# Node tiles of a two-layer graph network moved in small steps under its first layer, with a rebuilt first stage and a new layout of window sums

## The reference

```python
# layer 0: node-projected features are gathered by src, weighted by an edge MLP, summed by dst
f_s, f_v = project(x, Wl1_0, Wl1_1)                    # sc_s, sc_v: the same with Wsc0, Wsc1
w = gelu(gelu(ea8 @ Wfc1 / 8**.5) @ Wfc2 / 8) @ Wfc3 / 8          # 192 per edge: w0, w1, w2, w3
mid0, mid1 = w0*gs*y0, w3*(gv . y1)/3**.5              # gs, gv = f_s[src], f_v[src]; y = edge_attr_4
mid2, mid3 = (w1*gs)[..., None]*y1, w2[..., None]*gv*y0
mid_s, mid_v = segment_sum([mid0 mid1]), segment_sum([mid2 mid3])   # by dst, / 32**.5
res = sc + (mid_s @ Wa) * out(mid_s, mid_v)            # out: the projections Wl2_s, Wl2_v
x = layernorm(x + res)
# layer 1: s, v projected per node, gathered by dst, weighted by relu(ea64 @ W1) @ W2 (224),
# combined with the edge's unit direction (dot, outer and cross products), summed by src
agg = segment_sum(tp, src) / 32
fs, gate, gv = silu, sigmoid and gated vectors of agg @ W_out + skip
x = layernorm(x + concat(fs, gv))
```

## Time and profile before

| | us |
|---|---|
| median of 3 runs | 2745.41 (2740.61 to 2756.41) |
| the profiled execution | 2767.32 |
| its span in the trace | 2765.5 |

### The profile page before, as it was taken

One profiled execution on the slowest core, in us unless ns is written; L12 is line 12 of the kernel. 1 busy time (PEld: TensorE's weight loads), 2 busy tenths in 40 slices (PEclk: granted clock), 3 DMA queues, 4 the chain that ended last, 5 costly groups with the idle time before them and its releaser, 6 DMA issues.

```text
span 2765.5 us, 80992 instructions
## 1 busy us (share of the span) xinstructions
PE 2655.6 (96%) x24330; PEld 2250.7 (81%) x24330; DVE 1649.6 (60%) x4264; ACT 899.5 (33%) x2015; POOL 2063.6 (75%) x1856
## 2 busy tenths in 40 slices
PE   4799999999999999999999999999999999999996
PEld 2477777777777777979999999999999999999993
DVE  5365555556555555526666666666666666666664
ACT  1111111111111112224444444444444444444442
POOL 3477777777777775247888888888888888888884
PEclk9999799889989898659999999999999999999998
DMA  4343343333433333247888888888888888888877
GB/s 132 111 110 105 100 109 106 100 104 105 108 103 105 105 105 85 104 173 142 141 144 144 141 144 143 144 143 143 143 142 143 143 144 142 144 144 142 144 124 189
DMA packets 388993, 355.59 MB, mean 129 GB/s; under 512 B 60992, under 2 KB 340928, under 8 KB 388416
## 3 DMA queue, kind: packets, MB, share of 16 engines
q0 software_dynamic: 150528, 141.40, 34.9%
q1 hardware_dynamic: 234816, 209.69, 27.2%
q10 hardware_dynamic: 3616, 4.11, 0.6%
HBM read 244.75 MB, written 135.90 MB: 138 GB/s over the span
## 4 chain that ended last, share of the span: by engine, by line
PE 65%; POOL 16%; issue 11%; DMA 3%; DVE 1%; DVEq 0%; ACT 0%; SPq 0%; POOLq 0%; ACTq 0%
POOL gat L693 15%; PE ps_o L1062 13%; PE ps_w L1050 12%; PE ps_d L1071 10%; PE ps_o L1060 9%; PE ps_x L1084 6%; PE ps_g L909 4%; PE ps_x L1024 3%; DMA gat<-f,gidx 2%; PE ps_w L935 2%; PE ps_h L928 1%; PE ps_h L923 1%; PE ps_r L981 1%; DMA tab<-summed,sidx 1%; PE ps_y L998 1%
## 5 line engine op out<-in xcount | busy, mean ns | idle before, releaser
L740 POOL DMA_INDIRECT tab<-summed,sidx x784 | 1218.6, 1554 | 264.5 <-issue 212.7
L693 POOL DMA_INDIRECT gat<-f,gidx x784 | 751.8, 959 | 244.8 <-issue 232.0
L1291 DVE TENSOR_TENSOR prod<-ps_w,xg 128x768 f32<-128x768 f32 x392 | 375.4, 958 | 244.5 <-PE ps_w L1050 226.7
L1062 PE MATMUL ps_o<-ro_v,prod 128*128 128x96 f32 x3136 | 478.5, 275 | 0.0
L1062 PEld LDWEIGHTS ps_o<-ro_v,prod 128*128 128x128 f32 x3136 | 413.3, 192 | 0.0
L1050 PE MATMUL ps_w<-hid,wf 64*128 64x128 f32 x4704 | 369.3, 290 | 2.0 <-ACT hid L864 2.0
L863 ACT ACTIVATE xg<-ps_x 128x768 f32<-128x768 f32 x392 | 296.3, 808 | 198.8 <-PE ps_x L1084 189.4
L1050 PEld LDWEIGHTS ps_w<-hid,wf 64*128 64x128 f32 x4704 | 294.1, 188 | 70.2 <-issue 44.6
L1071 PE MATMUL ps_d<-msg,same 128*128 128x193 f32 x1568 | 332.5, 334 | 0.7 <-ACT summed L882 0.7
L1060 PE MATMUL ps_o<-ro_s,prod 96*128 96x96 f32 x1568 | 330.2, 292 | 0.6 <-DVE msg L1302 0.6
L909 PEld LDWEIGHTS ps_g<-sel,ta 128*128 128x128 f32 x1568 | 210.0, 209 | 95.0 <-issue 59.2
(11 more groups left out here) (198 smaller groups left out, 3416.9 us busy)
## 6 DMA issues: line engine op xcount, KB each, us to landing
src_bc<-in_src_rows SPq DMA_DIRECT2D x196, 256.0 KB
tabw<-feat SPq DMA_DIRECT2D x784, 36.0 KB
ea<-in_ea SPq DMA_DIRECT2D x196, 128.0 KB
feat<-fst SPq DMA_DIRECT2D x25, 576.0 KB, 2.9
gat<-f,gidx POOLq DMA_INDIRECT x784
hot_dst<-in_dst_rows SPq DMA_DIRECT2D x98, 128.0 KB
hot_dir<-sh_rows SPq DMA_DIRECT2D x98, 128.0 KB
dst_bc<-hot_dst SPq DMA_DIRECT2D x196, 64.0 KB
```

Source lines behind the costliest of these rows:

```text
L693: pool.indirect_dma_start(out=gat[:, r % 4, k, :], out_offset=None, in_=t["f0"], in_offset=bass.IndirectOffsetOnAxis(ap=gidx[:, r // 4, at ...
L740: pool.indirect_dma_start(out=t["tabs"][into[k]], out_offset=bass.IndirectOffsetOnAxis(ap=sidx[:, r, k:k + 1], axis=0), in_=summed[:, r, k ...
L1062: last = pe.matmul(ps_o[:, k, 96 + 64 * c:192 + 64 * c], prod[:, ur % 2, k, 1 + c, :], ro_v[:, c, :], start=True, stop=True)
L1291: dve.tensor_tensor(prod[:, r % 2, :, :, :].rearrange("p k c e -> p k (c e)"), ps_w4[:, :, 0:3 * P], xg[:, r // 2, r % 2 * 2:r % 2 * 2 + 2 ...
```

## The change

*Node tiles under the first layer.* The loops of PE and DVE in `fast()` take eight groups a step (`PER`), of which the first three steps are peeled. In each, one node tile is done in pieces: DVE copies its sums out of the accumulator (`node_parts`, r = 5, one step ahead), PE projects them (`update`, r = 0), DVE updates `xres` and computes the inverse root by a bit trick and three Newton steps, as a chain of linked one-column operations (`node_update`, `node_scale`, `node_norm`, r = 0, 1, 2), PE transposes and projects (r = 4, r = 6), DVE copies the rows out of PSUM (`node_turned`, `node_staged`). ACT spreads rows into `fst` in steps 2, 3, 4 of the next eight, and stores them to `feat` from its own queue. So tiles 0 to 22 are done within the loop. Of the last two, the sums follow the loop, and the rest stands in the peeled first steps of the second layer: norms at s = 0, transposes after the first gather, projections at s = 1 and 2, ACT's spreading at s = 3 and 4. SP stores the skip rows there (8 DMAs at g = 0, 2 at g = 1), and POOL's scatter of u = 1 waits for them; the tables are taken in a rotated order. One join is left. A tile may be read once no later group adds to it; `check_order` therefore adds to `win_ok` that each group's first target lies within 48 rows of an even spread.

*Sums.* One accumulator `acc` of five parts takes the place of three; DVE forms a dot product and a product with `y` itself (`vy`, `wy`, `dot`), so that `window_sums` has two products instead of three, and `add_window` one add instead of three.

*Unread matmuls.* At r = 1 of each eight groups PE issues four matmuls of 512 columns whose result is never read (`HOLD`); 16 more stand at the end of the first stage, where four stand at its start.

*First stage.* Weights come first in SP's queue, `x` and its transpose in five column chunks, PSUM has seven banks for the tiles, the index work stands at tiles 16 and 21 and behind them, and directions are computed in one pass. POOL issues the gathers of the first four groups there as soon as `f0` is stored. Memsets and loads for later stages move into this stage or into peeled steps of SP's loop: 9 + 8 + 18 + 6 weight loads and that of `sh` at groups 1, 3, 5, 7. DVE's one-time work of the node stage stands at groups 6, 8, 12, 14.

```diff
+PER = 8
+STEP = P // PER
+SLACK = 3
+TIN = (NGRP - 20) // PER + 1
+TSTAGE = (NGRP - 29) // PER + 1
+LAST = NT - 2
+ROOT_OPS = 16
...
+                pool.wait_ge(gidx_done, 1)
+                pool.wait_ge(f_out[0], 16 * (-(-NC // 2)))
+                pool.wait_ge(f_out[1], 16 * (NC // 2))
+                for u in range(4):
+                    for k in range(G):
+                        pool.indirect_dma_start(
+                            out=gat[:, u, k, :], out_offset=None, in_=t["f0"],
+                            in_offset=bass.IndirectOffsetOnAxis(ap=gidx[:, 0, u * G + k:u * G + k + 1], axis=0),
...
+                    if u % FT == 0:
+                        pe.wait_ge(xt_in[u // FT], 32)
+                    since(pe, f_ready, u - 6)
+                    since(pe, res_ready, u - 6)
+                    parts = ps_n[u % 7][:, 0:320].rearrange("p (k f) -> p k f", k=2)
...
+                    if isinstance(u, int) and u == 1:
+                        load_sums()
+                    if isinstance(u, int) and u == 3:
+                        load_nodes()
+                    if isinstance(u, int) and u == 5:
+                        load_hidden()
+                    if isinstance(u, int) and u == 7:
+                        load_out()
...
+                def store_skip(m):
+                    chunk = slice(m * FT, (m + 1) * FT)
+                    for h in range(2):
+                        sp.dma_start(tile_rows(t["tabs"][0], m)[:, :, 96 * h:96 * h + 96],
+                                     skip_at[:, chunk, h, :]).then_inc(skip_out, 16)
...
+                        for m in range(NC - 1):
+                            store_skip(m)
+                    if isinstance(g, int) and g == 1:
+                        sp.wait_ge(y_done, NT)
+                        store_skip(NC - 1)
+                    if isinstance(g, int) and g == 3:
+                        sp.wait_ge(feat_out, 16 * NT)
...
+                    tile = j * 2 + r // PER - 3
+                    if not isinstance(tile, int) or 0 <= tile < TSTAGE:
+                        if r % PER == 2:
+                            spread_rows(tile, 0)
+                        if r % PER == 3:
+                            spread_plus(tile, 0)
+                        if r % PER == 4:
+                            spread_minus(tile, 0)
+                            send_rows(tile, 0)
...
+                def send_rows(u, k):
+                    act.wait_ge(stage_done, u + 1)
+                    act.dma_start(t["feat"][bass.ds(u * P, P), :],
+                                  fst[:, k, :, :].rearrange("p c f -> p (c f)")).then_inc(feat_out, 16)
...
-                for n, (lhs, hi, lo, up) in enumerate(((ta, P, 0, 4), (tb, 96, 0, 1), (tc, 96, 1, 4))):
-                    for k in range(G):
-                        last = pe.matmul(ps_g[r][0:hi, (n * 4 + lo) * WIN:(n * 4 + up) * WIN],
-                                         lhs[:, r, k, :, :].rearrange("p a b -> p (a b)"),
-                                         sel[:, r, k, lo:up, :].rearrange("p a b -> p (a b)"),
-                                         start=k == 0, stop=k == G - 1)
+                for k in range(G):
+                    pe.matmul(ps_g[r][:, 0:4 * WIN], ta[:, r, k, :, :].rearrange("p a b -> p (a b)"),
+                              sel[:, r, k, :, :].rearrange("p a b -> p (a b)"), start=k == 0, stop=k == G - 1)
+                for k in range(G):
+                    last = pe.matmul(ps_g[r][:, 4 * WIN:5 * WIN], tb[:, r, k, :, :].rearrange("p a b -> p (a b)"),
+                                     ohot[:, r, k, :], start=k == 0, stop=k == G - 1)
                 last.then_inc(ready, 1)
...
+                def update(u):
+                    since(pe, y_done, u)
+                    pe.wait_ge(part_done, u + 1)
+                    node_sums(0, tile_sums[:, :, :])
...
+                def node_sums(k, sums):
+                    to_s, to_v = ps_p[:, 161 * k:161 * k + 65], ps_p[:, 161 * k + 65:161 * k + 161]
+                    pe.matmul(to_s, sums[:, 0, :], r_s[:, 0, :], start=True, stop=False)
+                    pe.matmul(to_s, sums[96:P, 4, :], r_s[96:P, 1, :], start=False, stop=True)
+                    pe.matmul(to_v, sums[0:96, 4, :], r_v[0:96, 0, :], start=True, stop=False)
+                    for c in range(3):
+                        last = pe.matmul(to_v, sums[:, 1 + c, :], r_v[:, 1 + c, :], start=False, stop=c == 2)
+                    last.then_inc(r_ready, 1)
...
+                            since(pe, acc_done, u - 1)
+                            if r == 1:
+                                idle_matmuls(pe, ps_g[ur % 2][:, :], ident[:, :], HOLD)
                             pe.wait_ge(sel_ready, u + 1)
                             pe.wait_ge(prod_done, u + 1)
-                            since(pe, acc_done, u - 1)
-                            window_sums(pe, ur, agg_done)
+                            window_sums(pe, ur % 2, agg_done)
...
+                            if r == 0:
+                                if isinstance(tile, int) and tile == 0:
+                                    pe.wait_ge(r_ok, 6)
+                                    pe.wait_ge(wn_in2, 16 * 8)
+                                update(tile)
+                            if r == 4:
+                                turn(tile, 0)
+                            if r == 6:
+                                project(tile, 0)
...
+                    gv = gat[:, r, :, S:D].rearrange("p k (c u) -> p k c u", c=3)
+                    dve.tensor_tensor(vy[:, :, :, :], gv, y[:, bass.ds(u * G, G), 1:4].unsqueeze(3).to_broadcast([P, G, 3, V]),
+                                      ALU.mult).then_inc(vy_done, 1)
+                    dve.wait_ge(w_ready, u + 1)
                     dve.tensor_tensor(ta[:, h, :, :, :], ps_w[h][:, :, 0:2 * S].rearrange("p k (a s) -> p k a s", a=2),
                                       gat[:, r, :, 0:S].unsqueeze(2).to_broadcast([P, G, 2, S]), ALU.mult)
-                    gv = gat[:, r, :, S:D].rearrange("p k (c u) -> p k c u", c=3)
-                    for dst, at in ((tb, 2 * S), (tc, 2 * S + V)):
-                        last = dve.tensor_tensor(dst[:, h, :, :, :],
-                                                 ps_w[h][:, :, at:at + V].unsqueeze(2).to_broadcast([P, G, 3, V]),
-                                                 gv, ALU.mult)
-                    last.then_inc(prod_done, 1)
+                    dve.tensor_tensor(wy[:, :, :], ps_w[h][:, :, 2 * S:2 * S + V],
+                                      y[:, bass.ds(u * G, G), 0:1].to_broadcast([P, G, V]), ALU.mult).then_inc(wy_done, 1)
+                    dve.wait_ge(vy_done, u + 1)
+                    dve.tensor_reduce(dot[:, :, :], vy[:, :, :, :].rearrange("p k c u -> p k u c"), AX.X, ALU.add).then_inc(dot_done, 1)
+                    dve.wait_ge(wy_done, u + 1)
+                    dve.tensor_tensor(tb[:, h, :, 0:3, :], wy[:, :, :].unsqueeze(2).to_broadcast([P, G, 3, V]), gv, ALU.mult)
+                    dve.wait_ge(dot_done, u + 1)
+                    dve.tensor_tensor(tb[:, h, :, 3, :], ps_w[h][:, :, 2 * S + V:2 * S + 2 * V], dot[:, :, :],
+                                      ALU.mult).then_inc(prod_done, 1)
...
+                def node_parts(u):
+                    settled(dve, r_ready, u, passed)
+                    here = bass.ds(u * P, P)
+                    dve.tensor_copy(tile_sums[:, :, :], acc[:, :, here]).then_inc(part_done, 1)
...
+                def node_scale(u, n):
+                    count = [0]
+                    def linked(ins):
+                        count[0] += 1
+                        ins.then_inc(ch_ln, 1)
+                        dve.wait_ge(ch_ln, u * ROOT_OPS + count[0])
+                    settled(dve, bs_done, u + n, passed)
+                    for k in range(n):
+                        last = dve.bn_aggr(mv[:, k, :], bst[:, k, :])
+                    linked(last)
+                    var, y, tmp = ntmp[:, 1, 0:n], rstd[:, 0:n], ntmp[:, 0, 0:n]
+                    linked(dve.tensor_scalar(var, mv[:, 0:n, 1], EPS, None, ALU.add))
+                    linked(dve.tensor_scalar(tmp.bitcast(I32), var.bitcast(I32), 1, None, ALU.logical_shift_right))
+                    linked(dve.tensor_scalar(y.bitcast(I32), tmp.bitcast(I32), -1.0, float(0x5f3759df), ALU.mult, ALU.add))
+                    for _ in range(2):
+                        linked(dve.tensor_tensor(tmp, y, y, ALU.mult))
+                        linked(dve.tensor_tensor(tmp, tmp, var, ALU.mult))
+                        linked(dve.tensor_scalar(tmp, tmp, -0.5, 1.5, ALU.mult, ALU.add))
+                        linked(dve.tensor_tensor(y, y, tmp, ALU.mult))
+                    assert count[0] == ROOT_OPS - 4
...
+                def node_turned(u, k, both=0):
+                    dve.wait_ge(tr_done, max(u + 1, both) if both else u + 1)
```

(38 more changed lines are left out.)

1004 lines of the change are left out of this document (505 added, 499 removed).

## The result

The changed kernel takes 3173.32 us (median of 4 runs, 3168.22 to 3178.79) against 2750.91 for the kernel before: a ratio of 1.1547, 95% interval 1.1509 to 1.1584. It is slower by 15%, where the forecast was 5% faster. The span of its profiled execution is 3169.9 us.

The account below looks back on a forecast made before the run. POOL's gather issue was taken to bound the first layer; node stage -133, start -18, gathers +7 and hand-over +13 sum to -131, so 2636 for the profiled execution and 2615 us at the median, range 2582 to 2665.

Parts of the forecast that it names:

- What bounds the kernel: First layer: POOL's issue of four indirect gathers a group, 1.25 us apart, sets the pace at 5.0 us a group.
- Is there room on PE?: First layer: PE at 4.34 us a group warm, 8.2 cold keeps POOL's 5.03 up to a cold share of 0.29.
- the formula: PE in the first layer: x/8.2 + (1-x)/4.34 >= 1/5.03, x being the share of time at 1.2 GHz.
- The rival of the slower side: First layer: PE's clock falls past break-even, cold half the time; at share 0.60 about 2815 us; chance 0.04.
- general path: Rival: data outside the 48-row bound, so 131 windows a group are swept, tens of milliseconds; chance 0.01.
- the ring: First layer: four buffers of gathered rows let POOL run ahead, covering up to three groups of DVE delay; cost 0.
- Two-port operations: DVE's small SBUF copies and scalings beside gathers: taken as nothing; rival, POOL locked out, 33 to 50 us, chance 0.12.
- Loads and one-time work: Gather loop: SP's 18 hidden-layer loads cost about 5, DVE's inverse norms 2; gathers +7, between -10 and +20.
- Start: First stage ends at 77 instead of 87.53, 17th gather at 92 instead of 110.02: -18 us.
- Hand-over: Last gather to first scatter: +4.4 before the join, +9 into the second layer; +13, between 0 and 25.
- Second layer: POOL's four scatters a group, 1.552 us each, a little over 7.4 us a group; steady state unchanged by the change.
- second row: Stretch from the 17th gather to the end of the last: 975.5 us before, 982.5 forecast.

Follow-up runs that it names:

- the last version: Changed kernel with 96-column second product, layer norm's end one group earlier, no wide matmuls, hidden-layer loads in six pieces, reciprocal in halves: 2704.93 us, 0.9871 of the kernel before.
- the run with early norm and no wide matmuls: Changed kernel with 96 columns in the second product, layer norm's end one group earlier on DVE, no unread 512-column matmuls: 2719 us.

## Why the prediction was wrong

*What bounds the kernel.* Right, and the experiments rest on it: POOL's issue is the bound as long as PE keeps up.

*Is there room on PE?* This is the step that failed, in three places. The sentence "I take the share as it was" is the main one: the share of time at 1.2 GHz was taken for a property of the stretch, 0.24, and it is a result of PE's own stream, which the change rewrote. It went to 0.66, and with the two products in the kernel before to all of the first layer. The rival had this case at 0.04, with the words "from 0.24 to 0.50 is far". The trace of before had the evidence for caution: within one to five groups at 1.2 GHz the clock came back each time while PE was busy without pause, so something in the stream brought it back, and the change altered the stream. Second, the rates: 16 matmul instructions for 24 were priced at a third less, 3.56 and 6.65 a group without node work, and they took 3.90 and 7.30. At 1.2 GHz a group of the kernel before is 8.15, 8.58 with the wider weights alone, and 7.30 with the third product gone as well: the wider weights cost 0.43 of the 1.28 that the third product had taken, and 0.85 was saved where 1.5 was priced. Third, the sum over both clocks: at a share of 0.66 the formula gives 6.3 us a group, and 7.6 were measured. It let PE make up in fast groups what it lost in slow ones. But a PE at 3.9 a group can only take what POOL's four buffers hold and then waits, so the time at 2.4 GHz is partly idle; worse, that very wait ended it.

*The wide matmuls.* That "whether they lift the clock, no row shows" was fair. They do lift it (the line at 574.18 above and the clock behind it), and the clock then lasts about three groups, until the next wait. Where the stream can do that itself, they only cost.

*The rival of the slower side.* It named the right mechanism, and its sign came true: POOL waits for DVE's products at most groups. Its price at a share of 0.60, 2815, was 360 too low, by the rates and the formula above for the most part; the share of 0.66 instead of 0.60 adds only some 50 by its own formula. (The 0.04 for slower leaves out the 0.01 of the general path, which would be slower too.)

*DVE.* Linked operations follow each other at 0.19, and the products as priced (busy 4.2 us a group in the last version, 4.4 priced). That "the ring covers up to three groups of that" was only half the story: POOL is covered by the ring, PE is not. PE's transposes wait for `x1b` in PE's own queue, with the next groups behind them, and at 3.9 a group PE reaches them 5 us early. The prediction listed who waits for DVE's products, and left this one out.

*Two-port operations.* Taken as nothing, with 33 to 50 as a rival, for copies and scalings. The cost exists and comes mostly from another operation. In the last version 155 of 692 gathers are longer than 1.0 us, 31.3 us over in sum against 9.9 in the kernel before, and all 155 begin while `sel`, `vy` or the part of `tb` made from `wy` is running, the three large products with both inputs in SBUF. Of the gathers that begin within one of the tile's own copies and scalings none is long. The size of the loss, 21 us more, is below the rival's, its place is another.

*Loads and one-time work.* The stall behind SP's 18 loads was priced at 5 and the reciprocal at 2; in the run with early norm and no wide matmuls PE waited 7.1 and 6.2 there, and taking both apart brought 14 us (2719 to 2705; the first is a single run, so the part of each stays open).

*Start.* The stage ended at 88.1, not 77: tiles started at 10.7 and kept their 1.66 us, which is the pitch at 1.2 GHz (the first two, at full clock, are 0.94 apart). The prediction took 1.66 over, and 1.2 as its hope (which makes 9 + 25 x 1.2 + 31 = 70, not 72), without asking at which clock the row stood; the clock column says 1.00 there in the kernel before. DVE's work behind the tiles took 25.6 (51.97 to 77.60) against 26 priced. The bound of 81 to 83 was the better half of that range, and then came the store, the memset and the end of the block with 10 instead of 5.

*Hand-over.* Priced at 46.2 from last gather to first scatter (13.1 + 20.1 + 13); 47.6 in the last version, and both of its parts come near their price: 19.0 to the join against 17.5, 28.5 behind it against 29.1. (The 4.4 of the first part is given as two times ten copies of 0.25, which would be 5.) In the changed kernel it was 68.6: POOL waits 38.9 us at the join for PE there, 19.0 in the last version, as PE brings its lag and its low clock along.

*Second layer.* "The change leaves that layer's steady state alone" missed 26 us. Two waits of 4.7 and 4.8 us for DVE's `sidx` stand in its first 35 us. The scatters take 1563 ns at the median instead of 1552, which is 9 over 784, and the rest is spread over many small waits for `sidx`. Why a scatter got longer wasn't tried and stays open; the rotated tables and the new places of the buffers are both in question.

Sum of the misses: second row +475.2, start +10.6, hand-over +22.4, second layer +26.0, end +1.3, which makes the 535.5 between 2634.4 and 3169.9.

## What to carry to other kernels

TensorE's clock is a result of the instruction stream, not a given of a stage: before pricing an edit of PE's stream, look at how the clock comes back in the trace after a fall, and ask if the new stream still has what brought it back. An edit that leaves PE fewer instructions can make it slower when it leaves fewer columns to stream and widens the weights under them; 72 unread columns on an existing matmul gave back 338 us, where more matmuls of their own did not. And a PE faster than its supplier does not bank time: it waits in a lump where its queue has the tightest dependence, so a pace is to be worked out with the buffers' depth, not as a mean.

## What the runs showed of the hardware

- The same kernel with 24 columns under 96-wide weights, with 24 under 128-wide ones, and with these and two products instead of three came back to 2.4 GHz from its cold start after about 28 us, after 175 us, and not at all; from 112 us of the trace on PE was busy without pause in all three. In the changed kernel, going from 24 to 96 columns brought it back after one or two groups of 7.3 us instead of not at all until the 512-column matmuls.
- The clock column of the profile can read 1.00 from the start of a trace on where all durations are those of 1.2 GHz (`layer1` 1.22 us from 100 to 120 us of the kernel before, and through 1400 us of the run with two products).
- A DVE product with both inputs in SBUF lengthens a POOL indirect transfer beside it, in the kernel before by up to 0.38 us (1326 against 946 ns); with one input in PSUM no such lengthening is seen (24 long ones against 45 without the product). It is the transfer that begins while the product runs which gets longer: 39 of 41 for `sel`, 39 of 45 and 0 of 60 for the added product with two inputs in SBUF and with one. The Trainium skill ("SBUF — State Buffer", Who interferes with whom) infers that `tensor_tensor` leaves descriptor generation alone, as it takes only the shared read side. The two runs here differ from that: +0.73% with both inputs in SBUF, 0.00% with one in PSUM. They agree with what the same section states of the rest, that a DVE instruction with two SBUF inputs contends with a GpSimd instruction that reads SBUF.
